# Score tasks between the blocks of the weighted sums, row scatters after them, and a step of GpSimd in another order

## The reference

```python
x = x + attn(layernorm(x))     # q, k, v = x@Wq, x@Wk, x@Wv in 16 heads of 8
                               # s = (q * 8**-0.5) @ k.T, causal; p = softmax(s); o = p @ v; o @ Wo + bo
x = x + ffn(layernorm(x))      # 8 experts of 128 -> 512 -> 128 with relu and biases
                               # probs = softmax(x @ gate_w.T); the 2 best experts, weighted by their probs
```

## Time and profile before

| | |
|---|---|
| time, median of 3 runs | 533.49 us (533.24 to 535.54) |
| span of the profiled execution | 527.7 us |
| own time of the profiled execution | not given beside its span |
| PE, DVE, ACT, POOL busy over the span | 89%, 78%, 68%, 54% |
| the 32 steps | about 47 to 352 us of the span, some 9.4 us a step in batch 0, some 10.2 in batches 2 to 5 |
| the expert part | about 352 to 527 us |

### The profile page before, as it was taken

The page is one execution under the profiler, slowest core; times in us unless marked ns, Lnnn a source line. Parts: engine busy times, 40 slices in busy tenths (PEclk is TensorE's granted clock), DMA queues, the critical chain, the costliest instruction groups (busy, mean ns, idle before and its releaser), DMA issues.

```text
span 527.7 us, 14330 instructions
## 1 busy us (share of the span) xinstructions
PE 469.7 (89%) x4121; PEld 328.0 (62%) x4121; DVE 413.1 (78%) x1519; ACT 358.9 (68%) x782; POOL 286.6 (54%) x579
## 2 busy tenths in 40 slices
PE   3788999999999999999999999989788789999981
PEld 1545656556555545546555545459688679999980
DVE  6898878988988888888888897875556555557875
ACT  7576877777867867876866857875456457777750
POOL 5603544535755766657657565725456555545542
PEclk9879999999999999999999999999999899999997
DMA  7434232132233233233333326722222322235653
GB/s 225 134 93 129 56 118 91 56 118 88 67 120 108 70 108 110 76 101 97 102 95 98 106 76 175 209 65 63 56 63 69 85 77 74 71 79 180 182 172 101
DMA packets 49454, 54.92 MB, mean 104 GB/s; under 512 B 6564, under 2 KB 41554, under 8 KB 49377
## 3 DMA queue, kind: packets, MB, share of 16 engines
q1 hardware_dynamic: 44736, 45.18, 29.5%
q0 software_dynamic: 4320, 8.47, 4.7%
q10 hardware_dynamic: 320, 0.36, 0.2%
HBM read 34.96 MB, written 17.90 MB: 100 GB/s over the span
## 4 chain that ended last, share of the span: by engine, by line
PE 50%; DVE 28%; ACT 7%; issue 7%; DMA 4%; another core or an unknown queue 3%; ACTq 1%; SPq 0%; POOL 0%; DVEq 0%; POOLq 0%
PE psO L1035 12%; DVE psS L1349 10%; PE psT L1197 7%; DVE maxs L1352 7%; PE psS L998 7%; PE psM L1208 5%; PE psO L1208 5%; PE psT L1011 3%; PE psS L1197 2%; ACT PT L811 2%; DMA xs_t<-sorted_x 2%; PE psS L1187 2%; DVE maxs L1349 1%; DVE xn L1278 1%
## 5 line engine op out<-in xcount | busy, mean ns | idle before, releaser
L811 ACT ACTIVATE PT<-psT 128x512 f32<-128x512 f32 x320 | 172.5, 594 | 67.6 <-PE psO L1035 45.0
L1349 DVE CUSTOM_DVE_ANT_0 psS<-mask_row,psS 128x512 f32<-128x512 bf16 (+1 forms) x232 | 142.8, 624 | 33.6 <-PE psS L998 29.3
L998 PE MATMUL psS<-Ks,Qs 96*128 96x128 bf16 (+3 forms) x512 | 132.9, 308 | 9.5 <-DVE maxs L1352 7.3
L598 POOL TENSOR_SCALAR_AFFINE_SELECT PT<-PT 128x512 f32<-128x512 f32 x124 | 76.8, 635 | 96.0 <-ACT PT L811 94.8
L1011 PE MATMUL psT<-Qs,Ks 108*128 108x384 bf16 (+3 forms) x512 | 109.9, 299 | 4.2 <-ACT PT L811 3.0
L695 POOL DMA_INDIRECT token_y<-Qs,y_row x71 | 70.8, 997 | 74.6 <-DVE Qs L1750 39.0
L998 PEld LDWEIGHTS psS<-Ks,Qs 96*128 96x128 bf16 x512 | 50.4, 99 | 53.5 <-DVE maxs L1352 26.4
L629 POOL DMA_INDIRECT sorted_x<-xn,place x64 | 64.3, 1005 | 27.6 <-issue 16.5
L1352 DVE TENSOR_REDUCE maxs<-psS 128x2 f32<-128x512 f32 (+3 forms) x120 | 75.7, 669 | 1.8 <-PE psS L1001 1.4
L1035 PE MATMUL psO<-PT,Vs 128*32 128x512 f32 (+3 forms) x1024 | 75.8, 436 | 0.3 <-DVE x_all L1375 0.3
L1011 PEld LDWEIGHTS psT<-Qs,Ks 108*128 108x128 bf16 x512 | 43.5, 97 | 32.8 <-ACT PT L811 12.9
(11 more groups left out here) (260 smaller groups left out, 741.1 us busy)
## 6 DMA issues: line engine op xcount, KB each, us to landing
Qs<-q_parts SPq DMA_DIRECT2D x96, 96.0 KB
Ks<-k_parts SPq DMA_DIRECT2D x95, 96.0 KB
xs_t<-sorted_x SPq DMA_DIRECT2D x71, 65.0 KB
w_sb<-in_L_ffn_w SPq DMA_DIRECT2D x16, 256.0 KB
k_parts<-kparts SPq DMA_DIRECT2D x8, 384.0 KB, 2.6
q_parts<-qparts SPq DMA_DIRECT2D x8, 384.0 KB, 3.6
x_all<-in_L_attn_x SPq DMA_DIRECT2D x8, 256.0 KB, 4.7
v_all<-token_y SPq DMA_DIRECT2D x4, 512.0 KB, 4.4
```

The lines of the kernel that those rows point to most:

```text
L598: pool.affine_select(out=square, in_=square, compare_op=ALU.is_ge, fill=0.0, base=0, pattern=[[0, GH], [1, P]], channel_multiplier=-1).the ...
L811: act.activation(PT[:, n * T:(n + 1) * T], psT[:, bank, :], ACT.Exp).then_inc(prob_done[bank], 1)
L998: last = pe.matmul(psS[:, bank, c0:c0 + n], Qs[0:QK_ROWS, g, h, j * P:n], Ks[0:QK_ROWS, g, h, 0:n], start=True, stop=alone)
L1349: dve.tensor_tensor_reduce(src, mask_row[:, (CH - 1 - j) * P:], src, 1.0, NEG, ALU.add, ALU.max, maxs[:, par, j, h:h + 1]).then_inc(scores ...
```

## The change

On PE, the four blocks of the weighted sums are no longer one stretch: score task 3 and probability task 2 stand behind block 0, score task 4 behind block 3, and the transposes of the maxima behind block 2. On ACT, the exponentials of task 2 stand ahead of the copy of the heads. On POOL, a step begins with the third part of k (step 0), then waits for the end of the weighted sums, copies the values, and issues the scatter that stood at the end of the step before; only then comes the first mask. The scatter in the middle of the step stands behind the first mask and, in step 3 (2 in the last batch), waits for the row counts.

```diff
             def step(b, g, first, last):             # POOL
                 s = b * GROUPS + g
+                masks = not (last and g == GROUPS - 1)
+                if g == 0 and AHEAD_QKV <= b + 1 < BATCH:
+                    third_k(b + 1)
+                if not (first and g == 0):
+                    weigh_over(s)                    # pool.wait_ge(pv_done, s)
+                if not (first and g == 0) and not (last and g > 0):
+                    pool.wait_ge(v_copied, b + (g + 3) // GROUPS + 1)
+                    load_v(b + (g + 3) // GROUPS, (g + 3) % GROUPS)
+                if b >= 2 and g > 0:
+                    scatter(b - 2, 3 * (g - 1) if last else 2 * (g - 1))
+                if b >= 3 and g == 0:
+                    scatter(b - 3, CH * TOPK - 2)
                 if last and g > 0:
-                    bank, turn = prob_turn(s, 2)
-                    pool.wait_ge(prob_done[bank], turn + 1)
+                    exps_over(s, 2)                  # the same wait
                     scatter(b - 2, 3 * g - 2)
-                masks = not (last and g == GROUPS - 1)
                 if masks:
                     mask(s, 0)
-                if not (first and g == 0) and not (last and g > 0):
-                    pool.wait_ge(pv_done, s)
-                    pool.wait_ge(v_copied, b + (g + 3) // GROUPS + 1)
-                    load_v(b + (g + 3) // GROUPS, (g + 3) % GROUPS)
-                if g == 0 and AHEAD_QKV <= b + 1 < BATCH:
-                    third_k(b + 1)
+                if b >= 2 and g == (2 if last else 3):
+                    pool.wait_ge(ranks_ready, b)
                 if b >= 2 and g > 0 and not last:
                     scatter(b - 2, 2 * g - 1)
-                if last and 0 < g < 3:
-                    scatter(b - 2, 3 * g - 1)
                 if b >= 3 and g == 0:
                     scatter(b - 3, CH * TOPK - 1)
+                if last and 0 < g < 3:
+                    if g == 1:
+                        exps_over(s, 6)
+                    scatter(b - 2, 3 * g - 1)
                 if masks:
                     mask(s, 1)
                     mask(s, 3)
...
-                if b >= 2 and not (last and g > 0):
-                    scatter(b - 2, 2 * g)
-                if last and 0 < g < 3:
-                    scatter(b - 2, 3 * g)
                 if last and g == 3:
                     scatter(b - 1, 0)
...
                 exps(s, 0)                           # ACT
                 exps(s, 1)
+                exps(s, 2)
                 if not (first and g == 0):
                     copy_heads(s - 1, (g + 3) % GROUPS)
...
                 for n in range(2, NPROB):
-                    exps(s, n)
+                    if n > 2:
+                        exps(s, n)
...
-                weighed(*KEY_BLOCKS)                 # PE
-
-                if nxt:
-                    turn_shift(s + 1, b + (g + 1) // GROUPS, (g + 1) % GROUPS)
+                weighed(KEY_BLOCKS[0])
                 sc(3)
                 if before:
                     probs(s, b, g, 2)
-                sc(4, 5)
+                weighed(*KEY_BLOCKS[1:3])
+                sc(4)
+                weighed(KEY_BLOCKS[3])
+                if nxt:
+                    turn_shift(s + 1, b + (g + 1) // GROUPS, (g + 1) % GROUPS)
+                sc(5)
                 probs(s, b, g, 3)
```

More of the change, by code:

```diff
@@ L631, in scatter, with weigh_over, exps_over @@
                     in_=xn2[:, b * CH + c, :], in_offset=None).then_inc(scattered[late_batch(b)], 16)
+            def weigh_over(s):
+                pool.wait_ge(pv_done, s)
+            def exps_over(s, n):
+                bank, turn = prob_turn(s, n)
+                pool.wait_ge(prob_done[bank], turn + 1)
             def step(b, g, first, last):
                 s = b * GROUPS + g
+                masks = not (last and g == GROUPS - 1)
[10 more added lines that the diff above has]
+                    scatter(b - 3, CH * TOPK - 2)
                 if last and g > 0:
-                    bank, turn = prob_turn(s, 2)
-                    pool.wait_ge(prob_done[bank], turn + 1)
+                    exps_over(s, 2)
                     scatter(b - 2, 3 * g - 2)
-                masks = not (last and g == GROUPS - 1)
                 if masks:
                     mask(s, 0)
-                if not (first and g == 0) and not (last and g > 0):
-                    pool.wait_ge(pv_done, s)
-                    pool.wait_ge(v_copied, b + (g + 3) // GROUPS + 1)
-                    load_v(b + (g + 3) // GROUPS, (g + 3) % GROUPS)
-                if g == 0 and AHEAD_QKV <= b + 1 < BATCH:
-                    third_k(b + 1)
+                if b >= 2 and g == (2 if last else 3):
+                    pool.wait_ge(ranks_ready, b)
                 if b >= 2 and g > 0 and not last:
                     scatter(b - 2, 2 * g - 1)
-                if last and 0 < g < 3:
-                    scatter(b - 2, 3 * g - 1)
                 if b >= 3 and g == 0:
                     scatter(b - 3, CH * TOPK - 1)
+                if last and 0 < g < 3:
+                    if g == 1:
+                        exps_over(s, 6)
+                    scatter(b - 2, 3 * g - 1)
                 if masks:
```

## The result

| | before | after |
|---|---|---|
| time, median of 4 runs each, run side by side | 533.8 us (533.24 to 535.54) | 543.71 us (541.47 to 544.25) |
| ratio, 95% interval | | 1.0188 (1.0156 to 1.022) |
| span of the profiled execution | 527.7 us | 542.3 us, its own time 544.05 |
| from W of step 1 to W of step 32 | 300.13 us | 310.16 us |

The change made the kernel 1.9% slower; the forecast was 525.0, 1.6% faster, with a range up to 533.5. The 31 steps between the first and the last W hold the loss: 10.03 us, against 9.9 between the medians. The spans differ by 14.6: besides these 10.0, the first W comes 1.7 later (49.18 for 47.49), and what stands behind the last W, nearly all of it the expert part, which the change leaves alone, took 180.1 us in the profile of before and 182.9 in this one. That part moves by several us from profile to profile, and by some 20 from chip to chip.

The account below looks back on a forecast made before the run. No engine is full: DVE's waits for score tasks and PE's waits for banks form a loop. Gains of 4 times 1.0 (batches 2 to 5), 1.75 and 2.8 make 8.55 us, so 525.0 us; range 514.5 to 533.5.

Parts of the forecast that it names:

- The sums' 2.18 us go by columns: Weighted sums on PE: the four blocks, split up, take 0.87, 0.65, 0.22 and 0.44 us by their columns.
- Nothing is added on PE, ACT or POOL but waits: The new order in each step costs these engines no extra work, only waits, such as 0.2 us before the heads' transposes.
- the 5.3: Sign of being wrong: score task 6 later than 5.3 us after the sums' begin in step 3; the round trip costs more.
- the forecast's gain of 8.55: Whole kernel: 8.55 us saved of the 527.7 us span, summed over all batches of the attention.
- Batches 0 and 1, seven steps with gaps but no scatters: 0.25 each: First two batches of the attention: each of seven steps gains 0.25 us, 1.75 in all.
- Slower: the heads' round trip decides: Rival: ACT's three exponentials run late, the heads' copy slips 0.5 us, 31 steps cost 7 us: 540.5 us; chance 0.11.
- The late signals belong to the sums' end: Rival: PE's late signals in steps 1 and 3 are not the scatters' doing and stay; 529 us; chance 0.12.
- the copy of the heads at 3.4 or later with no scatter beside it: Sign of being wrong, on ACT, in us after the sums' begin: the lateness is then not the scatters'.
- The scatters' step of the argument: A POOL scatter that begins while the sums end holds back PE's signals by 0.4 to 0.8 us.
- The third part of k: POOL's operation moved to the head of step 0: counted 0; bounds 0.7 us gained or 1.15 lost.
- The time around the span: Median lies 5.8 us above the profiled span; added to the forecast span of 519.1 us, giving 525.0.

Follow-up runs that it names:

- e8: The changed kernel with ScalarE's old order, the copy of the heads ahead of the exponentials of task 2; ratio to the kernel before 1.0219.
- e6: The kernel before with the change's GpSimd step, but the third part of k in its old place; ratio to the kernel before 0.991.
- e2: The changed kernel with GpSimd's old step, so only TensorE's and ScalarE's order changed; ratio to the kernel before 1.033.
- e13: The changed kernel run again, unaltered, beside the kernel before on a chip where that takes 507.01 us; ratio 1.0308.

## Why the prediction was wrong

**The step that failed: "The sums' 2.18 us go by columns".** The forecast priced each block, alone between full-width tasks, at its share of the unbroken stretch, and wrote "Nothing is added on PE, ACT or POOL but waits". No instruction is added, but four changes of width are. The forecast put them at nothing; they cost 0.45 us in each step, all ahead of the sums' end. With them the forecast's own schedule comes out as measured:

| after W, us | forecast | measured (step 2 of batch 3) |
|---|---|---|
| score task 3 | 0.87 | 1.00 |
| score task 4 | 2.18 | 2.54 |
| transposes of the maxima | 2.79 | 3.26 |
| copy of the heads | 3.04 | 3.51 |
| heads' transposes | 3.70 | 4.16 |
| score task 6 | 4.15 | 4.65 |

The last four are late by 0.46 to 0.50, and nothing makes up for it, because each waits for the one before. In step 3 score task 6 starts 5.59 after W (200.14), past the 5.3 that the forecast had named as a sign of being wrong. 31 steps at 0.45 are 13.95 us; the forecast's gain of 8.55 less these would be a loss of 5.4, and 10.0 was measured.

**The rest, 4.6 us, is mostly in the batches without scatters.** Less 0.45 a step, steps 1, 2, 3 and 0 of batches 3 and 4 would take 10.14, 9.66, 10.15 and 10.18. Against 10.33, 9.91, 10.30 and 10.35 before these are gains of 0.19, 0.25, 0.15 and 0.17, where the forecast had 0.21, 0.25, 0.36 and 0.2: only step 3 was put too high. Over the 16 steps of batches 2 to 5 these gains are 2.6 instead of 4.0, in the last eight 2.85 for 2.8.

But "Batches 0 and 1, seven steps with gaps but no scatters: 0.25 each" was wrong in sign. From the first W to the eighth the kernel before took 67.45 us and the changed one 72.11; less seven times 0.45 that is 68.96, a loss of 1.5 and not a gain of 1.75: 3.3 of the 4.6. A step of batch 0 took 9.36 to 9.44 us before, and the round trip asks for the sums' end and 6.85: with 2.79, 9.64. The later end was to be paid for by the scatters' delay that goes, and here there was none. VectorE's idle time was long (1.88 in the earlier trace rows) and yet did not set the step: the chain of the kernel before, from W of step 2 to W of step 3 (56.92 to 66.30), holds PE and 1.7 us of ScalarE (from 64.05 on), and no VectorE.

**The rivals.** "Slower: the heads' round trip decides" named the place and the sign, and the size nearly: 0.5 of slip, 540.5 us. Its trigger was wrong: the exponentials were in time (e8), and it was the sums that ended late. It had a chance of 0.11. "The late signals belong to the sums' end" was refuted by e6. The sign named for it, "the copy of the heads at 3.4 or later with no scatter beside it", did come (3.51 in the changed kernel), but from the sums' later end. The scatters' step of the argument held on the chips of the first kind: begun while the sums end, they hold back PE's signals, and without that steps 1 and 3 of batch 3 take 9.78 and 9.80 (e6) for 10.33 and 10.30.

But TensorE's new order does not seem to need GpSimd's new step for it: in e2, with the old scatters, the copy is at 3.51 after W as well (174.02 to 177.53, beside a scatter at 175.61). e2 ran on a chip of the second kind; on one of the first the copies of the first profile, but for the last, had started by 3.25, also ahead of 3.51, but e2 was not run there. So on the chips of the first kind the 10.0 us are what is left after this gain, and where the kernel before has little of the delay the same order costs the 15.9 of e13.

**The third part of k.** The forecast counted it at 0 with a bound of 1.15 lost if it met another operation of VectorE in its new place. It did, an operation that lasts 1.05 us, in the changed kernel too; there PE paces step 0 and it costs nothing (10.63 in the changed kernel and in e2), while in e1 it costs 0.7.

**The time around the span.** It is 1.75 us (544.05 less 542.3), not 5.8: by that the profiled execution of before took some 529.5, an estimate, less than the median. It did no harm, for the forecast is the median less 8.55 either way.

## What to carry to other kernels

Before matmuls of one width are cut up to let others in, look in the trace for what one change of width costs, start to start and in the weight loads, and multiply by the changes added; here two more, in the one step of four that VectorE paced, gave 0.2 us in batches 2 to 5, and four more in every step cost 0.45 us each time. Find which signal closes the loop: everything put ahead of it counts in full, even if the engine has idle time later. When a change has several parts, try them one by one, and on more than one chip: here GpSimd's part, with the third part of k left in its place, was worth 0.9% on one chip, while the whole of it gave nothing on two others, behind TensorE's part, which cost more everywhere it ran.

## What the runs showed of the hardware that was not expected

- A change of TensorE between narrow weights (12 or 32 columns) and full width, in either direction, costs 0.09 to 0.14 us in these kernels; from 32 to 12 columns it costs 0.02.
- A scatter issued by GpSimd while the sums end delays TensorE's signals to ScalarE and VectorE: at the copy of the heads in step 1 by 0.8 us in one profile (3.25 against 2.42 after W) and by 0.4 in another, on another chip (2.80). How it does so, and why it differs, no run shows.
- A small operation of VectorE on SBUF can last until GpSimd's operation beside it ends, and through two that follow each other: 1.05 for 0.16, 2.31 for 0.34 us. Others are not held up (0.34 beside a copy of the values).
- The expert part, the same instructions in all kernels, takes 160 to 164 us on the chips where the kernel before takes 507 us, and 178 to 185 on the others, while the changed kernel's attention is equal on both to 0.02 us. Why was not tried.
